# Random-feature attention block: key features from three full-height stacks, key norms as the bias of one exponential per head

## The reference, cut to what matters

```python
def feature_map(x, orf):                       # orf: 128 x 32
    proj = x @ orf.T / d_k ** 0.25
    norm = jnp.sum(x * x, axis=-1, keepdims=True) / (2.0 * math.sqrt(d_k))
    return (jnp.exp(proj - norm) + EPS) / math.sqrt(m)
q = feature_map(split(x @ Wq.T + bq), orf)
k = feature_map(split(x @ Wk.T + bk), orf)
v = split(x @ Wv.T + bv)
kv, ksum = jnp.einsum('nlm,nld->nmd', k, v), jnp.sum(k, axis=1)
out = (q @ kv) / (q @ ksum)                    # then Wo, layer norm, ternary product, layer norm
```

## Time and profile before

| | |
|---|---|
| time, median of 3 runs | 1302.82 us (1302.79 to 1304.18) |
| span of the profiled execution | 1300.4 us |
| granted TensorE clock | 0.998 of full speed |
| TensorE busy (matmuls) | 1280.2 us, 98% of the span |
| VectorE busy | 942.1 us, 72% |
| ScalarE busy | 702.1 us, 54% |
| GpSimd busy | 384.1 us, 30% |
| chain of work that ended last | PE 84%, DVE 6%, ACT 6%, issue 3%, DMA 1% |

### The profile page before, as it was taken

How to read it: one execution, slowest core, us unless ns; L and a number is a source line. 1 busy time by engine, 2 the same in 40 slices (tenths; PEclk the granted TensorE clock), 3 DMA queues, 4 the chain that set the end, 5 groups by cost and what they waited for, 6 DMA issues and landing times.

```text
span 1300.4 us, 24924 instructions
## 1 busy us (share of the span) xinstructions
PE 1280.2 (98%) x8626; PEld 965.9 (74%) x8626; DVE 942.1 (72%) x1784; ACT 702.1 (54%) x1403; POOL 384.1 (30%) x685
## 2 busy tenths in 40 slices
PE   9999999999999999999999999999999999999987
PEld 8767787777877678776787768876788767887665
DVE  7599765886668875787657786587875787657876
ACT  5557435564355743657336663367534665446534
POOL 1213432125311343214421234312352123422143
PEclk9999999999999999999999999999999999999999
DMA  7668414773146821567215762258612686026711
GB/s 242 140 136 217 95 50 111 170 190 84 57 118 160 200 68 54 133 159 189 62 57 130 182 165 69 62 130 197 162 45 71 142 209 149 30 80 147 163 51 65
DMA packets 83773, 160.56 MB, mean 123 GB/s; under 512 B 19648, under 2 KB 37184, under 8 KB 83136
## 3 DMA queue, kind: packets, MB, share of 16 engines
q1 hardware_dynamic: 67856, 139.78, 43.4%
q10 hardware_dynamic: 9648, 16.85, 3.4%
q0 software_dynamic: 6144, 2.34, 2.1%
HBM read 39.13 MB, written 16.78 MB: 43 GB/s over the span
## 4 chain that ended last, share of the span: by engine, by line
PE 84%; DVE 6%; ACT 6%; issue 3%; DMA 1%; POOL 0%; SPq 0%; ACTq 0%; DVEq 0%; POOLq 0%
PE ps L943 28%; PE ps L980 25%; PE ps L1044 8%; PE ps L1012 4%; PE ps L966 4%; PE ps L968 4%; PE ps L967 4%; PE ps L999 4%; ACT features L687 2%; PE ps L1070 2%; ACT x_hi L655 1%; DMA rows<-in_Wk_t 1%; DVE squares_turned L853 1%; ACT unit_hi L668 0%; DVE cols L857 0%
## 5 line engine op out<-in xcount | busy, mean ns | idle before, releaser
L687 ACT ACTIVATE features<-ps 128x512 f32<-128x512 f32 x512 | 279.0, 603 | 254.4 <-PE ps L943 196.0
L584 POOL DMA_DIRECT2D stacks<-norm_rows x128 | 86.3, 681 | 305.7 <-DVE norm_rows L868 185.8
L943 PE MATMUL ps<-Wo_hi,stacks 128*128 128x512 f32 x448 | 150.4, 402 | 0.0
L660 ACT ACTIVATE values_then_attention<-ps 128x512 f32<-128x512 f32 x64 | 38.3, 598 | 197.2 <-PE ps L968 194.1
L809 DVE TENSOR_TENSOR den<-den,features 128x512 f32<-128x512 f32 x186 | 128.0, 688 | 12.7
L562 POOL TENSOR_SCALAR stats<-stats 128x1 f32<-128x1 f32 x128 | 36.1, 282 | 323.4 <-DVE stats L796 323.2
L943 PE MATMUL ps<-orf_key_a,stacks 128*128 128x256 f32 x512 | 131.4, 288 | 0.1
L943 PE MATMUL ps<-orf_key_b,stacks 68*128 68x256 f32 x512 | 128.2, 282 | 0.0
L1044 PE MATMUL ps<-features,kv_ksum 128*32 128x512 f32 x1024 | 123.1, 598 | 3.4 <-ACT features L687 2.1
L845 DVE SCALAR_TENSOR_TENSOR unit_lo<-ps,cols,unit_hi 128x512 fp32r<-128x512 f32 x128 | 94.2, 736 | 35.0 <-ACT squares L670 34.9
L943 PEld LDWEIGHTS ps<-orf_key_a,stacks 128*128 128x128 f32 x512 | 97.1, 190 | 25.9 <-issue 22.1
(11 more groups left out here) (141 smaller groups left out, 2773.2 us busy)
## 6 DMA issues: line engine op xcount, KB each, us to landing
stacks<-unit_hi SPq DMA_DIRECT2D x384, 128.0 KB, 2.4
stacks<-unit_lo SPq DMA_DIRECT2D x256, 128.0 KB, 3.7
stacks<-unit_hi SPq DMA_DIRECT2D x64, 256.0 KB, 3.9
out<-rows ACTq DMA_DIRECT2D x56, 256.0 KB, 2.0
rows<-in_x_t SPq DMA_DIRECT2D x49, 256.0 KB, 4.5
rows<-in_x SPq DMA_DIRECT2D x32, 256.0 KB, 4.3
features<-in_x SPq DMA_DIRECT2D x32, 256.0 KB, 4.2
values_then_attention<-in_x_t SPq DMA_DIRECT2D x8, 256.0 KB, 7.1
```

What stands on the lines that cost most here:

```text
L584: pool.dma_start(slot[row:row + 2, c:c + L].rearrange("o (t c) -> o t c", c=DH), NN[2 * DH * p:2 * DH * (p + 1), u % 2, part, :].bitcast(F ...
L687: nc.scalar.activation(FE[:, n % 8, :, 0:M], ps[:, :].rearrange("p (a m) -> p a m", a=HG), ACT.Exp, scale=C_EXP).then_inc(a_exp.sem, 1)
L943: last = mm(out, a, b, start=(n == 0), stop=(n == len(terms) - 1))
```

## The change

The four products of a key tile become three. `ST` is split into a key stack of 3 x 1024 columns (KST) and a query stack (QST). The twelve 32-row pieces that the four heads need (hi, lo and hi again, against the rounded and the rest part of the matrix) fill three stacks of exactly 128 rows; stack n holds pieces of heads n and n + 1, and its product covers their 256 columns, so that the three overlap by one head in PSUM. SyncE's key copies go from 10 to 9, with the same bytes.

No room is left for the rows of norms. Key norms are now summed with their sign turned into KN (token by head), written by GpSimd to device memory, and read back with four copies in another order into NB (one column per head and tile). The exponential takes that column as its bias, which holds for one head only: one exponential of 128x512 becomes four of 128x128. PE no longer waits for key norms; ScalarE does, at the first key tile. Queries keep their way.

```diff
-                        for p in range(2):
-                            at_a, at_b = L * p + P * r, L * (2 + p) + P * r
-                            last = products(ps[:, 256 * p:256 * (p + 1)], [(slot[:, at_a:at_a + P], MA[:, :]),
-                                                                          (slot[0:KK, at_b:at_b + P], MB[0:KK, p, :])])
+                        for n in range(3):
+                            last = mm(ps[:, M * n:M * (n + 2)], KST[:, L * n + P * r:L * n + P * (r + 1)], MK[:, n, :],
+                                      start=(n == 0), stop=(n == 2), skip_group_check=True)
...
-                    nc.scalar.activation(FE[:, n % 8, :, 0:M], ps[:, :].rearrange("p (a m) -> p a m", a=HG),
-                                         ACT.Exp, scale=C_EXP).then_inc(a_exp.sem, 1)
+                    if is_key(u):
+                        if r == 0:
+                            norms_lifted(act, b, u)
+                        for h in range(HG):
+                            last = nc.scalar.activation(FE[:, n % 8, h, 0:M], ps[:, M * h:M * (h + 1)], ACT.Exp,
+                                                        bias=NB[:, h, r:r + 1], scale=C_EXP)
+                        last.then_inc(a_exp.sem, 1)
...
+            def turn_key_norms(b, u):
+
+                there = by_head[u // 2 % 2]
+                wait(v_ns.sem, v_ns.nth(b, 2 * u + 2))
+                pool.dma_start(there.rearrange("h t a r -> (h t) a r"), KN[:, :, :]).then_inc(n_spilled.sem, 16)
+                wait(n_spilled.sem, n_spilled.nth(b, u // 2 + 1))
+                if b or u:
+                    wait(a_exp.sem, a_exp.nth(b, 8 * (u - 1)))
+                for a in range(4):
+                    pool.dma_start(NB[DH * a:DH * (a + 1), :, :], there[:, :, a, :].rearrange("h t r -> t h r")).then_inc(n_lifted[0].sem, 16)
...
+                    if is_key(u):
+                        for n, r, h, k in ((0, 2 * DH, 0, 2), (1, DH, 1, 2), (2, 0, 2, 2), (0, 0, 0, 1), (2, 3 * DH, 3, 1)):
+                            sp.dma_start(slot[r:r + DH * k, L * n:L * (n + 1)], hi[DH * h:DH * (h + k), :]).then_inc(sig.sem, 16)
+                        wait(v_plo.sem, v_plo.nth(b, 2 * u + 2))
+                        for h, (n, r) in enumerate(((0, DH), (1, 0), (1, 3 * DH), (2, 2 * DH))):
+                            sp.dma_start(slot[r:r + DH, L * n:L * (n + 1)], lo[DH * h:DH * (h + 1), :]).then_inc(sig.sem, 16)
...
+                    if is_key(u):
+                        if h == 0:
+                            dve.wait_ge(n_spilled.sem, n_spilled.nth(b, u // 2))
+                        by_tile = KN[:, :, 4 * h:4 * (h + 1)].rearrange("p a t -> p t a")
+                        nc.vector.reduce_sum(by_tile, blocks.rearrange("p (t a) c -> p t a c", a=4),
+                                             axis=mybir.AxisListType.X, negate=True).then_inc(v_ns.sem, 1)
...
-                elif kind == "N":
+                elif kind == "N" and not is_key(u):
...
-                for r in range(4):
-                    a = r // 2
-                    nc.vector.tensor_copy(MA[DH * r:DH * (r + 1), M * a:M * (a + 1)], wT[DH * r:DH * (r + 1), 0:M])
+                for n, r, a in ((0, 0, 0), (0, 1, 0), (0, 3, 1), (1, 0, 0), (1, 2, 1), (1, 3, 1), (2, 1, 1), (2, 2, 1)):
+                    nc.vector.tensor_copy(MK[DH * r:DH * (r + 1), n, M * a:M * (a + 1)], wT[DH * r:DH * (r + 1), 0:M])
```

More of the change, by code:

```diff
@@ L274, in attention_kernel @@
         TQ, NT = sb("squares_turned", [P, HALF]), sb("norms_turned", [P, DH])
-        NN = sb("norm_rows", [P, 2, 2, DH], F32R)
+        NN = sb("norm_rows", [P, 2, DH], F32R)
+        KN, NB = sb("key_norms", [P, 4, TT]), sb("key_bias", [P, HG, TT])
+        by_head = nc.dram_tensor("norms_by_head", (2, HG, DH, 4, TT), F32, kind="Internal").ap()
         DR = sb("den", [P, 2, HALF])
@@ L578, in lift_norms @@
                     wait(t_ff.sem, t_ff.nth(b, 0))
-                wait(v_n.sem, v_n.nth(b, 3 * u + 3))
+                wait(v_n.sem, v_n.nth(b, 3 * (u // 2) + 3))
                 for part in range(2):
-                    if is_key(u):
-                        for p in range(2):
-                            row, c = 2 * DH + 2 * part, L * (2 + p)
-                            pool.dma_start(slot[row:row + 2, c:c + L].rearrange("o (t c) -> o t c", c=DH),
-                                           NN[2 * DH * p:2 * DH * (p + 1), u % 2, part, :].bitcast(F32))\
-                                .then_inc(n_lifted[0].sem, 16)
-                    else:
-                        row = 3 * DH + part
-                        pool.dma_start(slot[row:row + 1, :].rearrange("o (t c) -> o t c", c=DH),
-                                       NN[:, u % 2, part, :].bitcast(F32)).then_inc(n_lifted[1].sem, 16)
+                    row = 3 * DH + part
+                    pool.dma_start(slot[row:row + 1, :].rearrange("o (t c) -> o t c", c=DH),
+                                   NN[:, part, :].bitcast(F32)).then_inc(n_lifted[1].sem, 16)
+            def turn_key_norms(b, u):
[7 more added lines that the diff above has]
+                    pool.dma_start(NB[DH * a:DH * (a + 1), :, :], there[:, :, a, :].rearrange("h t r -> t h r")).then_inc(n_lifted[0].sem, 16)
             for kind, b, at, _, _ in steps():
                 t = at[0] if at else 0
-                if kind == "NL":
+                if kind == "NL" and is_key(t):
+                    turn_key_norms(b, t)
+                elif kind == "NL":
                     lift_norms(b, t)
@@ L742, in constant_columns @@
             def constant_columns():
-                dve.wait_ge(s_k, 5)
+                dve.wait_ge(s_k, 3)
                 dve.wait_ge(s_ld, 16 * 3)
-                nc.vector.tensor_scalar(ABC, BC, A_SQ, None, ALU.mult)
+                for k, scale in enumerate((A_KEY, A_QUERY)):
+                    nc.vector.tensor_scalar(ABC[:, k:NU:2], BC[:, k:NU:2], scale, None, ALU.mult)
                 for k in range(KT):
@@ L763, in constant_rows @@
                     nc.vector.tensor_tensor(WQS[r, h, :], wT[r, 0:M], rounded[r, :].bitcast(F32), ALU.subtract)
[L764 to L771 removed]
+                for n, q, a in ((0, 2, 0), (1, 1, 0), (2, 0, 0), (2, 3, 1)):
+                    r = slice(DH * q, DH * (q + 1))
+                    nc.vector.tensor_tensor(MK[r, n, M * a:M * (a + 1)], wT[r, 0:M], rounded[r, :].bitcast(F32), ALU.subtract)
+                nc.vector.tensor_copy(WQS[3 * DH:QK, :, :], minus_one).then_inc(s_orf, 1)
             def weight_scale():
@@ L998, in _ @@
                         c = L * h + HALF * half
-                        last = mm(ps[:, :], WQS[0:QK, h, :], slot[0:QK, c:c + HALF], start=True, stop=True)
+                        last = mm(ps[:, :], WQS[0:QK, h, :], QST[0:QK, c:c + HALF], start=True, stop=True)
                     last.then_inc(t_f.sem, 1)
```

88 lines of the change are left out of this document (37 added, 51 removed).

## The result

The changed kernel takes 1336.22 us (median of 4 runs, 1332.33 to 1342.86) against 1303.19 us before in the same session: ratio 1.026 (95% interval 1.022 to 1.029). It is slower by 33 us where the forecast was 5.9 us faster. The profiled execution took 1332.47 us and spans 1330.6 us, 30.2 more than the span of before. Its mean granted TensorE clock is 0.992 of full speed, against 0.998: worked out from the spans, that is 10.6 us lost to the lower clock against 2.6, so up to 8 of the 30.2 us are clock (up to, since a low clock costs nothing while TensorE waits).

A forecast was written before the change was run, and what follows sets the result against it. TensorE, 98% busy, was taken to bound the kernel, with ScalarE's spare time as the local question. Terms -30.7 + 14.7 + 3.2 + 2.8 + 3.5 + 0.6 = -5.9 on 1302.8 gave 1296.9 us, range 1287 to 1312.

The forecast's parts named there:

- prologue: Before the first key unit: VectorE makes 8 instead of 4 small copies and TensorE waits for it, +0.6 us.
- Key norms: Write and read back: both landings take 5.4 us where 7.2 is allowed, in time by 1.8, so no cost.
- the walk: Queues followed from a key unit's first tile: norms' write starts at 14.4 us, TensorE feels late norms at 24.2.
- B: Rival, chance 0.20: norms late in units 2, 4 and 6; landings of 4.4 each cost 3.7 us a batch, 1326.
- Short exponentials: On ScalarE, four 128x128 exponentials a key tile at 0.255 us each, 1.02 a tile, 136 us more in all.
- A: Rival, chance 0.17: smaller stalls, exponentials 0.23 us apart, about 9.5 us more gained, 1287 to 1292.
- C: Rival, chance 0.18: short exponentials on ScalarE overlap less; 1304.6 us at 0.275 apart, 1315 at 0.295.
- Units 2 and 4: ScalarE's queue stays ahead of TensorE, slacks 0.9 us or more: nothing lost, 0.96 saved a unit, 15.4 in all.
- Unit 0: Two store stages of 1.18 us fill ScalarE; TensorE waits 2.1 at the fourth query tile, 14.7 over seven units.
- The saving itself: On TensorE, three products for four spare 0.12 us a key tile, 0.96 a unit, 30.7 over 32 key units.
- Unit 6: ScalarE held by x loads, GpSimd 1 to 2 us later for x_lo: 0.4 us lost each, 2.8 over seven.
- Last batch: Unit 6 there, without covering projections: G tiles start 2.6 us later, 3.5 us lost with the saving.

The follow-up runs named there:

- e1: The changed kernel with a constant column as the exponentials' bias, so nothing waits for the key norms, whose copies are still made: 1309.32 us, ratio 1.005.
- e4: The changed kernel with the reads taking norms an earlier key unit wrote, so nothing waits for the write to land: 1304.35 us, ratio 1.001.
- e2: The changed kernel with one 128x512 exponential without bias per key tile, norms copied but waited for by nobody: 1279.05 us, ratio 0.981.
- e10: The changed kernel with x loads and stores moved later, and batch 0's weight passes moved from unit 0 to unit 1: 1299.07 us, ratio 0.997.
- e7: The changed kernel with key norms written and read back in two halves, ten GpSimd copies a unit in place of five: 1329.6 us, ratio 1.020.
- e8: The changed kernel with key norms in two halves and the two store stages moved from unit 0 to unit 1: 1314.11 us, ratio 1.008.
- e11: The changed kernel with the norms' write and reads issued by SyncE, behind the same unit's lifts, in place of GpSimd: 1344.92 us, ratio 1.031.
- e12: e10 with the norms' write and reads issued by SyncE in place of GpSimd: 1334.38 us, ratio 1.024.
- e6: The changed kernel with the two store stages of the batch before moved from unit 0 to unit 1: 1325.83 us, ratio 1.018.
- e9: The changed kernel with x loads moved from the end of unit 2 to unit 3's and stores from unit 0 to unit 1: 1300.97 us, ratio 0.998.
- e5: The changed kernel with the next batch's five x loads moved from the end of unit 2 to the end of unit 3: 1316.31 us, ratio 1.009.

## Why the prediction was wrong

By spans, the forecast lay 36.1 us under the measured one (1330.6 against 1296.9 - 2.4). By stretch, forecast and measured:

| stretch | forecast | measured | missed by |
|---|---|---|---|
| prologue | +0.6 | +1.0 | 0.4 |
| unit 0 to 2 | 7 x (2.1 - 0.96) + (3.2 - 0.96) = +10.2 | +17.7 | 7.5 |
| unit 2 to 4 | -7.7 | -6.8 | 0.9 |
| unit 4 to 6 | -7.7 | +15.6 | 23.3 |
| unit 6 to 0 | 7 x (0.4 - 0.96) = -3.9 | -1.6 | 2.3 |
| last unit 6 | +2.5 | +4.3 | 1.7 |

- **Key norms, the step that failed.** The forecast put them at nothing: both landings at twice 2.7, 5.4 us, in time by 1.8. In batch 3 they took 9.2, and late norms with what they set off cost 21.3 us (e1). The rest of the walk was good: write at 15.0 for 14.4, then 0.7 to the first read, 1.7 to the last, and 9.2 make 26.6, which is 2.4 over the walk's limit of 24.2, and TensorE waited 2.44. What was wrong is the choice between the two groups of the earlier trace rows. The write took 3.4 (median), the last of the four reads 5.3 to 6.7 in the five late batches. The place should have decided, not the shape: I named the x loads as evidence for B, yet took a median over all units for a step whose transfers run beside 1.3 MB of loads. Rival B had the mechanism right, and unit 4 as the tightest place; but it spread the loss over units 2, 4 and 6 of every batch, where the runs show it in unit 4 and mostly in the five batches 1 to 4 and 6. Unit 2 kept its 0.98 us in most batches. B's time also lacked the clock, 1.7 us in three batches.
- **Short exponentials, right.** 0.25 apart against 0.255 taken. Neither A nor C came. The Trainium skill's estimate ("ScalarE: Activation LUTs", What ACT_TABLE_LOAD costs) of 0.29 is not what these rows show; the measurement decides.
- **Units 2 and 4 as far as ScalarE goes, right** in batches 1 to 6: -0.98 in unit 2 in most of them, and -0.98 in unit 4 where norms were in time (e1, e4).
- **Unit 0, the right engine and stages, two terms small.** The store stage is 1.41 and not 1.18, because the next exponential starts 0.44 after the DMA's issue began and I had added only durations. And the walk stopped at the fourth query tile, while the backlog went on to the last pair of query exponentials. The miss is 0.8 us a batch, of which the two store stages give 0.46 and the saving that isn't had there (next point) 0.23; that is 5.6 in all, and 1.9 more in batch 0, where the clock dip after the 2.86 us wait was not foreseen.
- **The saving itself was credited too widely.** About 0.96 us came only from unit 2 on and from unit 4 on. e2 gives 0.73 in unit 0: its first projection product starts 1.0 us after the unit's start as before, so the first two tiles' 0.24 is not had. It gives 0.6 to 0.9 in the later units 6; why less isn't known. In batch 0 it gives 0.18 from units 2 and 4, and from the last batch's unit 4 it is 0.36 slower than before: TensorE waits for VectorE's unit_lo there, 0.55 us in batch 0 and 1.16 in the last, which my slacks, taken from other batches, didn't have.
- **Unit 6.** The forecast saw GpSimd late for x_lo; the larger effect was its additions beside VectorE's splits.
- **Last batch.** In the changed kernel TensorE waits 1.45 and 0.54 us from 1263.7 on, and the granted clock is at 0.50 for 6.9 us from 1264.2 on. e4 and e10, whose clock stays at 1.00 there, lie at +2.2 and +2.3, near the forecast's +2.5; that the clock is the whole difference isn't shown.

With the longest landing of the earlier trace rows, 6.0, for just one of the two, the sum of both is 8.7, and B's own arithmetic gives 3.4 us a batch, about 1324. That would have been nearer by luck, since it takes the time from three units a batch; from unit 4 alone it gives 12 us, 1309.

## What to carry to other kernels

- When an edit puts a round trip through memory ahead of a consumer, price it at the place where most other traffic runs, not by a median over the kernel, and add what a TensorE stall does to its own clock.
- Before a step moves to another engine or queue, list what stands behind it there and by when each must be issued: four of twelve kernels here (e7, e8, e11, e12) only moved the wait.
- Fix causes together before judging them: e6 alone made its neighbour worse by 8 us, and the pair of reorderings (e9) turned a loss of 33 us into a gain of 2.

## What the hardware showed that I had not expected

- TensorE's granted clock was at 0.50 for 3.4 to 3.5 us with waits of 2.44, 2.98 and 3.32 us in unit 4 and of 2.86 us in batch 0, and stayed at 1.00 with waits of 2.86 and 2.40 us elsewhere. With the same wait of 2.8 to 2.9 us in batch 0 it was low for 3.4 us in e4 and e6 and for 6.8 in e1, e5, e9 and e11. The length of the wait alone doesn't tell; what does is open.
- Reads of 4 KB issued by GpSimd land in 1.7 us at best, and in 4.1 to 5.9 us in batch 3's unit 4, beside loads of 256 KB.
- VectorE's fp32 splits took 3.47 us for two beside GpSimd's additions, and 1.28 us without.
- SyncE took 0.43 us to issue each small read whose pieces are 32 bytes (e11, e12); GpSimd took 0.56.
